# A graph attention and GRU kernel: new orders in the first GRU layer, layer norm statistics moved to the second, and a first stage rebuilt

## The reference

```
h = max(layernorm(x), 0)
Wh = h @ W;  e = leaky(Wh@a1 [:,None] + Wh@a2 [None,:]);  e = where(adj > 0, e, -9e15)
x = x + elu(softmax(e) @ Wh)
h = max(layernorm(x), 0)
for i in range(3):
    aggr = A^T (h @ weight[i])            # A = (adj != 0)
    gi, gh = aggr @ w_ih.T + b_ih, h @ w_hh.T + b_hh
    r, z = sigmoid(i_r + h_r), sigmoid(i_z + h_z);  n = tanh(i_n + r*h_n)
    h = (1-z)*n + z*h
x = x + h
```

## Time and profile before

| what | us |
|---|---|
| median of 3 runs | 689.55 |
| the profiled execution, its own time | 689.75 |
| its span in the profile | 687.9 |
| TensorE (PE) busy | 623.6 (91%) |
| VectorE (DVE) busy | 539.0 (78%) |
| ScalarE (ACT) busy | 451.9 (66%) |
| GpSimd (POOL) busy | 255.4 (37%) |

### The profile page before, as it was taken

How to read it: one execution, slowest core, us unless ns; L and a number is a source line. 1 busy time by engine, 2 the same in 40 slices (tenths; PEclk the granted TensorE clock), 3 DMA queues, 4 the chain that set the end, 5 groups by cost and what they waited for, 6 DMA issues and landing times.

```text
span 687.9 us, 8791 instructions
## 1 busy us (share of the span) xinstructions
PE 623.6 (91%) x2845; PEld 458.4 (67%) x2845; DVE 539.0 (78%) x1234; ACT 451.9 (66%) x777; POOL 255.4 (37%) x263
## 2 busy tenths in 40 slices
PE   2686999998999899998999989998999999999995
PEld 2465776676686676776766766766767776767774
DVE  4767998599876998779985998769987699648545
ACT  2784787477874778566875778647785677554443
POOL 1203544246241461525432453414715234413440
PEclk9799899999999999999999999999999999999998
DMA  6521131023202132022410132021320122001001
GB/s 222 183 93 62 62 121 32 33 61 123 92 31 92 33 123 92 15 79 61 146 39 32 62 123 92 30 81 44 122 93 6 56 87 67 1 1 30 1 1 30
DMA packets 28669, 47.39 MB, mean 69 GB/s; under 512 B 1672, under 2 KB 19408, under 8 KB 28624
## 3 DMA queue, kind: packets, MB, share of 16 engines
q1 hardware_dynamic: 28624, 46.84, 21.0%
HBM read 42.60 MB, written 4.23 MB: 68 GB/s over the span
## 4 chain that ended last, share of the span: by engine, by line
PE 55%; DVE 26%; ACT 8%; issue 5%; POOL 5%; DMA 1%; DVEq 0%; ACTq 0%; POOLq 0%
PE ps_x L970 14%; PE ps_g L1008 10%; PE ps_x L951 6%; DVE score L665 5%; DVE zh L757 3%; ACT score L389 3%; PE ps_r L1017 2%; DVE zh L764 2%; PE ps_z L1018 2%; PE ps_z L1017 2%; PE ps_r L1019 2%; PE ps_r L1018 2%; PE ps_z L1019 2%; DVE hkT L751 2%; DVE nn L744 2%
## 5 line engine op out<-in xcount | busy, mean ns | idle before, releaser
L1008 PE MATMUL ps_g<-edges,h_hi 128*128 128x512 f32 x384 | 157.7, 411 | 10.6 <-DVE h_lo L773 9.2
L1008 PE MATMUL ps_g<-edges,h_lo 128*128 128x512 f32 x384 | 152.2, 396 | 0.0
L389 ACT ACTIVATE score<-score,nmax 128x1024 f32<-128x1024 f32 x64 | 73.8, 1153 | 48.1 <-DVE nmax L665 47.1
L970 PE MATMUL ps_x<-probT,h_nat 128*128 128x512 f32 x224 | 98.9, 594 | 0.0
L1008 PEld LDWEIGHTS ps_g<-edges,h_hi 128*128 128x128 f32 x384 | 73.1, 190 | 29.0 <-DVE h_lo L773 12.8
L665 DVE CUSTOM_DVE_ANT_0 score<-score,away 128x1024 f32<-128x1024 f32 x64 | 86.6, 1353 | 7.3 <-ACT score L383 6.5
L300 POOL TENSOR_SCALAR tz<-tz 128x512 f32<-128x512 f32 x32 | 24.6, 769 | 172.9 <-ACT tz L430 172.9
L275 POOL TENSOR_SCALAR rstd<-mv 128x4 f32<-128x4 f32 (+1 forms) x24 | 9.9, 412 | 199.4 <-DVE mv L707 146.9
L1008 PEld LDWEIGHTS ps_g<-edges,h_lo 128*128 128x128 f32 x384 | 73.2, 191 | 14.0
L396 ACT ACTIVATE probT<-ps_x 128x512 f32<-128x512 f32 x128 | 70.9, 595 | 17.2 <-PE ps_x L951 17.1
L951 PE MATMUL ps_x<-ident,score 128*128 128x128 f32 x512 | 71.0, 281 | 11.4 <-ACT score L389 10.0
(11 more groups left out here) (136 smaller groups left out, 1331.5 us busy)
## 6 DMA issues: line engine op xcount, KB each, us to landing
adj_in<-in_adj SPq DMA_DIRECT2D x64, 512.0 KB, 3.3
x_nat<-in_x SPq DMA_DIRECT2D x8, 512.0 KB, 4.3
ej<-ej_kept_at SPq DMA_DIRECT2D x8, 512.0 KB, 3.4
out<-nn SPq DMA_DIRECT2D x16, 256.0 KB, 2.3
probT<-in_L_gnn_weight SPq DMA_DIRECT2D x1, 192.0 KB
probT<-in_L_gnn_w_ih SPq DMA_DIRECT2D x1, 192.0 KB
probT<-in_L_gnn_w_hh SPq DMA_DIRECT2D x1, 192.0 KB
ej_kept_at<-ej_row SPq DMA_DIRECT2D x8, 4.0 KB
```

Source lines behind the costliest of these rows:

```text
L389: act.activation(score[t % U][:], score[t % U][:], ACT.Exp, bias=nmax[:, t:t + 1], scale=-1.0, accum_out=rowsum[:, t:t + 1]).then_inc(exp_ ...
L970: last = pe.matmul(bank_of("agg", c, par)[:], h_nat[par][:, j, :], probT[:, j, :], start=(j == 0), stop=(j == T - 1))
L1008: last = pe.matmul(ps_g[c][:], part[:, s, :], edges[par][:, s, cols(c)], start=(s == 0 and part is h_hi), stop=(s == T - 1 and part is h_lo))
```

## The change

Steady passes. Layer 0: VectorE's order changes (statistics out, the first low part ahead, `n_input` of half 0 ahead of the scores of tile 2, `n_input` of half 1 in two parts with `lo_half` between, conversions of edges later), and TensorE's (the first transposes of the attention ahead of `h_back` of the pass before, z ahead of r, `h_back` of half 0 ahead of the last product of half 1, `h_back` of half 1 in the middle of a `neighbours`). ScalarE's order in layer 0 stays, but for `h_tiles`. Layer 1 takes `norm1` and `rstd1`. `dots` goes from layer 1 to layer 2 in two parts, `h_tiles` to the end of layer 1 and into layer 2, `away_tile` of tile 1 to the end of the pass.

First stage. x of graph 0 comes in two halves, and its statistics go by halves; the weights come on ScalarE's queue; ej is spread by TensorE (a transpose of a column broadcast) instead of through DRAM; the casts of the weights go behind the loop over tiles and mostly to ScalarE; one copy of each tile from tile 2 on goes from ScalarE to VectorE; four of the eight conversions of edges, the layer norm's relu of graph 1 and the weight products go behind the loop.

```diff
 sync:
-            sp.dma_start(x_nat[0][:], x_v[0]).then_inc(x_loaded, 16)
...
+            for c in range(2):
+                sp.dma_start(x_nat[0][:, c * TH:(c + 1) * TH, :], x_v[0][:, c * TH:(c + 1) * TH, :]).then_inc(x0_loaded[c], 16)
+            for t in range(2):
+                sp.dma_start(adj_in[t][:], adj_v[0, t]).then_inc(adj_loaded[t], 16)
...
-            spread_ej(0, 0, True)
             for t in range(TA, T):
                 load_adj(0, t)
             for t in range(TA):
                 load_adj(1, t)
             spread_ej(1, 1)
 gpsimd:
             def first():
-                rstd1(0)
+                first_rstd1(0)
+                first_rstd1(1)
                 rstd1(1)
                 rstd2_half(0, 0)
+                rstd2_half(0, 1)
                 split_h(0, 0, 0)
-                rstd2_half(0, 1)
                 split_h(0, 0, 1)
             def body(b, par, attend, prepare):
-                if prepare:
-                    rstd1(b + 2)
                 for l in range(L - 1):
                     z_times_h(b, l, 0)
+                    if prepare and l == 1:
+                        rstd1(b + 2)
                     z_times_h(b, l, 1)
 scalar:
+            def first_ej_half(c):
+                act.wait_ge(wide_ps, c + 1)
+                act.activation(ej[:, cols(c)], ps_x[c][:], ACT.Copy).then_inc(wide_done, 1)
+            def setup_weights(n):
+                dst, bk = ((wT[:, F:(1 + L) * F], ps_r), (wihT, ps_z), (whhT_hi[:], ps_in))[n]
+                act.wait_ge(setup_pe, 4 + n)
+                act.activation(dst, bk[:, 0:3 * F], ACT.Copy).then_inc(setup_act, 1)
+            def setup_layer_hi(l):
+                act.wait_ge(setup_pe, 7 + l)
+                act.activation(cT_hi[:, l, :], (ps_r, ps_z, ps_in)[l][:, 0:3 * F], ACT.Copy).then_inc(setup_act, 1)
             def first():
+                load_weights()
                 h_tiles(0, 0, 0)
                 h_tiles(0, 0, 1)
-                row_of_ej(0, 0)
+                first_ej_half(0)
+                first_ej_half(1)
                 leaky_tile(0, 0, 0, True)
                 for t in range(T):
                     if t + 1 < T:
                         leaky_tile(0, 0, t + 1, True)
                     if t >= 1:
-                        probT_tile(0, 0, t - 1)
+                        probT_tile(0, 0, t - 1, [0] if t >= 3 else [0, 1])
                     exp_tile(0, t)
-                    if t == 2:
-                        h_tiles(1, 1, 0)
-                        h_tiles(1, 1, 1)
-                    if t == TH + 2:
+                    if t == TH + 1:
                         aggT_half(0, 0, 0, True)
-                probT_tile(0, 0, T - 1)
                 elu_exp(0, 0)
+                probT_tile(0, 0, T - 1, [0])
+                h_tiles(1, 1, 0)
+                aggT_half(0, 0, 1, True)
+                h_tiles(1, 1, 1)
+                elu_exp(0, 1)
+                h0_half(0, 0, 0)
+                for n in range(3):
+                    setup_weights(n)
+                h0T_half(0, 0, 0)
+                h0_half(0, 0, 1)
                 row_of_ej(1, 1)
-                aggT_half(0, 0, 1, True)
-                h0_half(0, 0, 0)
-                elu_exp(0, 1)
-                h0T_half(0, 0, 0)
+                for l in range(L):
+                    setup_layer_hi(l)
+                h0T_half(0, 0, 1)
                 leaky_tile(1, 1, 0)
-                h0_half(0, 0, 1)
-                leaky_tile(1, 1, 1)
-                h0T_half(0, 0, 1)
-                act.wait_ge(setup_dve, 12)
+                act.wait_ge(setup_dve, 9)
             def body(b, par, attend, prepare):
+                if b == 0:
+                    g_hi_half(b, 0, 0)
+                    leaky_tile(a, a_par, 1)
                 if attend:
                     exp_tile(a, 0)
-                g_hi_half(b, 0, 0)
+                if b > 0:
+                    g_hi_half(b, 0, 0)
...
# h_tiles(b + 2, par, 0): from behind leaky_tile(a, 4), layer 0, to behind leaky_tile(a, 7), layer 1
# h_tiles(b + 2, par, 1): from behind leaky_tile(a, 6), layer 1, to behind g_hi_half(b, 2, 1), layer 2
 vector:
+            def first_norm1(c):
+                dve.wait_ge(x0_loaded[c], 16)
...
+            def first_probT(t):
+                dve.wait_ge(probT_ps, 2 * t + 2)
+                dve.tensor_copy(probT[:, TH:T, tile_cols(t % TH)], ...).then_inc(probT_dve, 1)
...
+            def dots_of(b, par, k, dst):
+                for t in range(T):
+                    last = dve.scalar_tensor_tensor(dot[:, k, t, :], h_nat[par][:, t, :], 1.0, w_rep[:, k, :], ALU.mult,
+                                                    ALU.mult, accum_out=dst[:, t:t + 1])
+                last.then_inc(e_done, 1)
             def first():
-                norm1(0, 0)
+                first_norm1(0)
+                first_norm1(1)
                 setup_projections()
-                dots(0, 0)
-                setup_gates()
+                ... first_dots by halves: ej, ej, ei, ei
+                away_tile(0, 0, 0)
                 norm1(1, 1)
-                away_tile(0, 0, 0)
-                edge_tile(0, 0, 0)
                 for t in range(T):
                     scores(0, t)
                     if t + 1 < T:
                         away_tile(0, 0, t + 1)
-                        edge_tile(0, 0, t + 1)
-                setup_layer(0)
-                setup_layer(1)
+                    if t < TA:
+                        edge_tile(0, 0, t)
+                    if t >= 3:
+                        first_probT(t - 1)
+                setup_gates()
                 att_half(0, 0, 0, True)
+                first_probT(T - 1)
                 x1_half(0, 0, 0)
-                dots(1, 1)
                 att_half(0, 0, 1)
+                x1_half(0, 0, 1)
                 split_h0(0, 0, True)
-                x1_half(0, 0, 1)
-                setup_layer(2)
+                setup_gates_lo()
+                dots_ej(1)
+                edge_tile(0, 0, TA)
+                edge_tile(0, 0, TA + 1)
                 split_h0(0, 1, True)
+                edge_tile(0, 0, TA + 2)
+                edge_tile(0, 0, TA + 3)
+                dots_ei(1, 1)
+                setup_layer_lo(0)
+                setup_layer_lo(1)
+                setup_layer_lo(2)
                 away_tile(1, 1, 0)
+                away_tile(1, 1, 1)
             def body(b, par, attend, prepare):
                 ...                                # out_half(b - 1, 0), or scores(a, 0) where b == 0
-                    away_tile(a, a_par, 1)
+                g_lo_half(b, 0, 0)
                 if b > 0:
                     out_half(b - 1, a_par, 1)
                     scores(a, 1)
-                    norm1(b + 2, par)
-                g_lo_half(b, 0, 0)
                 g_lo_half(b, 0, 1)
-                    edge_tile(a, a_par, 0)
+                n_input(b, 0, 0)
                     away_tile(a, a_par, 2)
                     scores(a, 2)
-                n_input(b, 0, 0)
+                new_h(b, 0, 0)
+                    edge_tile(a, a_par, 0)
+                r_times_hn(b, 0, 1)
+                lo_half(b, 0, 0)
+                add_in(b, 0, 1)
                     edge_tile(a, a_par, 1)
-                new_h(b, 0, 0)
+                new_h(b, 0, 1)
+                    away_tile(a, a_par, 3)
                     edge_tile(a, a_par, 2)
-                n_input(b, 0, 1)
-                lo_half(b, 0, 0)
-                new_h(b, 0, 1)
-                    away_tile(a, a_par, 3)
                 lo_half(b, 0, 1)
-                    edge_tile(a, a_par, 3)
                     scores(a, 3)
+                    edge_tile(a, a_par, 3)
...
                 n_input(b, 1, 0)
+                    norm1(b + 2, par)
                 new_h(b, 1, 0)
                     away_tile(a, a_par, 6); edge_tile(a, a_par, 6); scores(a, 6)
-                    dots(b + 2, par)
...
                 g_lo_half(b, 2, 1)
+                    dots_ej(b + 2)
                     split_h0(a, 0)
+                    dots_ei(b + 2, par)
                     away_tile(b + 2, par, 0)
+                    away_tile(b + 2, par, 1)
 tensor:
+            def wide_half(c):
+                pe.wait_ge(first_ej, c + 1)
+                for t in range(c * TH, (c + 1) * TH):
+                    last = pe.transpose(ps_x[c][:, tile_cols(t % TH)], ej_col[:, t:t + 1].broadcast_to([P, P]), ident[:])
+                last.then_inc(wide_ps, 1)
+            def first_agg_tile(t, par=0):              # in place of first_agg_pair, two tiles at a time
+                for j in range(T):
+                    if j % TH == 0:
+                        pe.wait_ge(*prob_count(0, t, j // TH))
+                    last = pe.matmul(bank_of("agg", t // TH, 0, True)[:, tile_cols(t % TH)], h_nat[par][:, j, :], ...)
             def hn_of_h(b, l, c):
-                if l == 0 and c == 0:
-                    pe.wait_ge(out_done, b * 2 + 1)
```

(73 more changed lines are left out.)

214 lines of the change are left out of this document (117 added, 97 removed).

## The result

The changed kernel takes 712.21 us (median; 711.39 to 712.75), the kernel before 689.5 us in the same runs: ratio 1.0329, 95% interval 1.0311 to 1.0347. It is 3.3% slower. I had forecast 701.7 with a range up to 711: the direction held, the size was about half of it, and the time lies above the range.

What follows compares the result with a forecast made beforehand. TensorE, 91% busy, was taken as the bound, with layer 0's chain on VectorE, ScalarE and GpSimd. Terms -1.5 + 0.3 + 5.5 + 3.0 + 4.8 = +12.1 us gave 701.7 on the median, range 684 to 711.

Steps and rivals of the forecast that it cites:

- r gate: Layer 0, ScalarE: the r gate runs 5.65 to 6.35 us after the last h, only 1.15 us before the old one.
- The scores of tile 2 end at 243.35: Layer 0, VectorE: behind n_input's wait for the r gate, mask 0.65 and scores 1.25 us end at 243.35.
- Half 1, 0.8 a pass, bounds 0.2 to 1.4: Layer 0, half 1: later lo_half makes TensorE reach the 257.94 point 0.2 to 1.4 us later, 0.8 taken.
- my lower case: Layer 0, half 1: with no GpSimd collision lo_half ends at 254.2, and TensorE is 0.2 us later.
- Statistics out of layer 0, -2.2 a pass: Layer 0: taking the statistics out alone, in the old order, is worth about 2.2 us a pass.
- Layer 1, +0.3: Layer 1: the moved statistics delay the attention and h_back, costing 0 to 0.6 us a pass, 0.3 taken.
- Seventh pass +3.0: Seventh pass: no statistics to lose but the new order, 15.5 instead of 13.54 us plus half 1's delay: +3.0.
- The clock, +4.8: TensorE's clock falls after a 3.3 us wait in layer 0: 0.8 us a pass for six passes, +4.8.
- First stage, keeps 1.5: First stage and first pass: most of a 9.6 us lead is lost, partly on ej's trip; 1.5 us kept.
- (2): Rival, all six passes: clock falls and both VectorE operations are caught by GpSimd; +24.7 at most, about 708; chance 0.13.
- (3): Rival, first stage: the row of ej is not held, 7 us kept there, kernel gains 3.5: 686; chance 0.12.
- (4): Rival, layer 0: takes 13.5 us like the old seventh pass, because the r gate is early enough: 678; chance 0.10.

Runs made afterwards that it cites:

- e3: Changed kernel with GpSimd's z times h of half 0 in layer 0 waiting for the scores of tile 2: 704.48 us, ratio 1.0217.
- e4: Kernel before with only the statistics chain moved out of layer 0, all orders of layer 0 and the first stage kept: 679.14 us, ratio 0.9846.
- e8: Changed kernel with 12 filler matmuls more a pass in TensorE's wait before h_back of half 0: 710.98 us, ratio 1.0313.
- e7: e1 with graph 1's ej sent earlier: transpose ahead of the weight products, DMAs ahead of the last two adjacency loads: 680.41 us, ratio 0.9869.
- e1: Changed kernel with VectorE's mask and scores of tile 2 back ahead of n_input of half 0 in layer 0: 684.09 us, ratio 0.9912.
- e5: e1 with VectorE's order of half 1 in layer 0 put back as before, TensorE's new order kept: 682.82 us.

## Why the prediction was right in direction and too small

- **r gate.** Forecast 5.65 us after the last h; measured 245.03 - 239.39 = 5.64. VectorE's wait: forecast 2.75, measured 2.83. Right.
- **The scores of tile 2 end at 243.35 (9.65 us after the last h).** This is the step that failed. They end at 10.62: 1.0 us later, for the collision with GpSimd's product (2.20 us instead of 1.23). I had moved n_input ahead of the scores on VectorE without asking what GpSimd does in the new place: the z gate releases it in the same moment. I priced the collision only where the trace of before showed it, at the mask of half 1. e3 gives the size, 7.7 us in seven passes, about 1 of it the two longer passes behind a fall of the clock; my sum had 0 for the collision.
- **Half 1, 0.8 a pass, bounds 0.2 to 1.4.** This step failed too. Layer 0 in all took 2.7 us more than before in the second pass (22.84 against 20.18). Without the scores' 1.0 that leaves 1.7, above my upper bound. I had looked for the collision with GpSimd's split at the mask and the edge conversion, and had taken `new_h` of half 1 at its usual length. The trace shows the mask at 0.68, the conversion at 1.10 and the last step of `new_h` at 1.68 instead of 0.69. Without any collision I had lo_half end 20.5 us after the last h; with 1.0 for the scores, 1.0 for `new_h` and 0.4 for the conversion that is 22.9, measured 22.8. So the order itself cost about what my lower case said, and the collisions the rest. TensorE's new place for h_back does not show in it: add_in starts right behind lo_half, without a wait for its product.
- **Statistics out of layer 0, -2.2 a pass.** Right: e4. **Layer 1, +0.3.** The second neighbours to layer 2 take 21.3 us after and 21.6 before, so 0.3 less, not more. (GpSimd's power chain takes 3.6 us, 238.96 to 242.57 in the third pass before, not the 5 that I gave it; it cost nothing.) **Layer 2, 0.** Measured 0.2 a pass.
- **Seventh pass +3.0**, measured 4.5; the same two terms. **Eighth 0**, measured 0.4.
- **The clock, +4.8.** Wrong in size, the other way: about 1.2 (e8). The falls came as read from the earlier trace rows, but the slow stretch lies in front of another wait. This error hid a part of the other.
- **First stage, keeps 1.5.** It lost 3.1 with the first pass. Every station up to the row of ej was right within about 1 us. The trip of ej was 10.1 us where I had taken 7, and the scores of tile 2 took 2.20 us in the first pass too (e3's first pass ends 0.5 us sooner). e7 shows that the trip was on the path.
- **Rivals.** (2) had the nearest sum, 708 or more, with VectorE operations caught by GpSimd as its kind of cause, but it put the loss on other operations and most of it on the clock. (3) named the place (the row of ej) where a gain could have come from; (4) did not come: layer 1's neighbours start 17.5 us after the last h, not 13.5; the r gate at 5.64 was late enough to hold the scores.

By its terms: forecast -1.2 + 5.5 + 3.0 + 4.8 = 12.1; measured 3.1 + 14.4 + 4.5 + 0.4, the clock's 1.2 among them, and 0.4 less behind the last h = 22.1 of span. The forecast had the direction by the right wait, the r gate in front of the scores. That the clock was taken 3.6 us too high, and so covered about a quarter of what the other terms missed, is luck. What stays open: the collision in half 1 is read from the traces; no run took it away by a wait on GpSimd, as e3 did for the scores, and VectorE's and TensorE's orders of half 1 were undone only in e1's setting, not under the late n gate.

## What to carry to other kernels

In a hand-written order, moving a waiting instruction ahead of work that other engines need costs the wait and everything queued behind the released work: write down, per engine, what stands behind it, and look also at what the same event releases on GpSimd, and which VectorE operation will then run beside it. A time won by one engine is worth what the next engine's list can take up; look for the stage before (here the scores of tile 1 and ScalarE's list) that does not move. When undoing one order gains nothing, undo its partner with it before calling it harmless, and compare the lengths of the same operation in both traces: here 0.3 us of order decided whether the operation on the path or the one behind it was caught.

## What was not expected of the hardware

The scores operation took 2.20 us beside a GpSimd product and 1.23 apart from it, and the product 1.84 instead of 1.26; an added wait that kept them apart gained 7.7 us in the kernel. It looks as if both lose, but the rows tell it in order. The product and VectorE's mask start together at 247.09: the mask keeps its 0.69, and the product ends 0.6 us late, at 248.93. The scores start at 247.81, beside the product, and end at 250.01, 1.1 after it, about the length that they have alone. In e5 the product takes 1.84 too, beside an edge conversion and with no scores near. In the same way `new_h` of half 1 (258.33 to 260.01) ends 0.6 us after GpSimd's split (257.84 to 259.45), which keeps its 1.6. So in these pairs the one that is first keeps its length, and the other's work comes nearly whole behind it.

A 4 KB DMA issued behind four or two loads of 512 KB took 4.4 and 3.7 us between its issue and the issue of its follower, against 1.2 with none ahead (58.51 and 59.73 in SyncE's timeline before). TensorE at half speed for some us in passes 2 to 7 cost about 1.2 us in all.
